# One core of Trainium2: where the row maxima are transposed between two thirds of the keys' product in an attention phase

## The chip, the cores and the metric

The kernel runs on one core of a Trainium2 chip. The metric is the device time of one execution in microseconds (us).

## The reference, cut to what matters

A decoder layer on x of shape (4, 512, 512): causal attention with 16 heads of 32, a first expert layer chosen by token id, a second expert layer with a router (2 of 8) beside a shared one, each with a residual and a layer norm. The change lies in the attention:

```python
qkv = x @ w_attn + b_attn
q, k, v = jnp.split(qkv, 3, axis=2)
...
att = jnp.einsum('bhqd,bhkd->bhqk', q, k) * (1.0 / np.sqrt(hs))
att = jnp.where(causal, att, -jnp.inf)
att = jax.nn.softmax(att, axis=-1)
y = jnp.einsum('bhqk,bhkd->bhqd', att, v)
...
x = _layernorm(x + _L0_attn_ref(x, L0_attn_w_attn, L0_attn_b_attn, L0_attn_w_proj, L0_attn_b_proj), axis=-1)
```

## The kernel before

The attention is cut into 16 groups of four heads of one batch element (NG = B * G = 16; group g belongs to batch element g // 4). Each product in float32 is made of three parts with numbers split in a high and a low half (hi x hi, lo x hi, hi x lo), four matmuls of 128x512 each, so a product has three thirds ("parts" 0, 1, 2), all at L482.

The order of the whole phase is one list of steps that attention_steps writes out. Every engine walks the same list and issues its own share of each step, so the order of each engine follows from the list, and semaphores join them. The kinds of step that matter here:

- **Q, K** (group g, part): the product of queries or keys into a bank of psT. After the last part ScalarE adds the bias and rounds to the high half (L624, ch_hi), VectorE subtracts to get the low half (L766, ch_lo) and frees the bank. Then 12 DMA copies (L362, on the sync engine's queue; for the keys of the first three groups some are issued by ScalarE, L631 and L635) bring the halves into the stacks qS and kS of the group. There are three of each stack, but one ch_hi and one ch_lo, with a half for Q and a half for K. ScalarE overwrites the Q half for group g only when all copies of group g - 1 have landed (stack_in).
- **P1** (group, unit u = 0 to 9): the scores, queries down the partitions, into psS (L548); VectorE masks them and takes the row maxima (L782). The first unit of a group waits for the landing of its stack, each later one for the maxima of the unit two before.
- **M** (group): four transposes of the row maxima into four rows of a psT bank (L556). ScalarE writes them, negated, as four more rows of qS (L642).
- **P2** (group, unit): scores again, keys down the partitions, with the maxima subtracted by those four rows, into psE (L569); ScalarE's exponential (L652); GpSimd's causal mask (L424).
- **PV** (group, j): numerators and denominators into psO and psN (L587). NORM and YH divide and split the result. V, PR, XT, CW, LN1, LN2 (L833), ST, LZ and ZB are the values' product, the output product with its layer norm and stores, the loads of the residual and the transposes of weights for the next phase.

XT, Q, K, V, PR, M and CW share the two banks of psT by turns: every use takes the other bank from the one before, in the order of the list (a product at its part 0), and waits until the last use of that bank is read (sh_free).

Pass s of the loop (16 of them) runs P1 of group s + 1 beside P2 of group s and PV of group s - 1. Its start, called "head s" in this document, is made of the six parts of Q and K of group s + 2; from the fourth on, a unit of P1 of group s + 1 stands after each, and M of group s stands after one of them. In the heads 14 and 15 there is no product of that kind, and M follows two units of P1, or none.

After the head come four PV steps (from s = 1 on) with units of P1 and P2 between, then the remaining units spread over V or PR products. The fourth pass of each batch element and the third have no such product to fill with.

The two waits that the step M has on TensorE:

```python
elif kind == "M":
    g = s[1]
    out = take(s)
    pe.wait_ge(max_done, UNITS * (g + 1))
    for t in range(QT):
        last = pe.transpose(out[0:4, t * P:(t + 1) * P], rowmax[:, g % 2, t, :], ident[:])
```

Of the kernel before, what the change touches and what calls it, by code (L numbers as in the profile page):

```python
# [24 lines left out]
def attention_steps(B, QT, NG):  # L25

    def product(kind, *at):
        return [(kind, *at, part) for part in range(3)]

    def spread(slots, extra):  # L30
        out, taken = [], 0
        for n, s in enumerate(slots):
            out += s
            upto = len(extra) * (n + 1) // len(slots)
            out += extra[taken:upto]
            taken = upto
        return out

    steps = []
    for i in range(QT):  # L40
        steps += [("XT", 0, i)]
    steps += product("Q", 0) + product("K", 0) + [("RT1",)]
    steps += product("V", 0, 0) + [("CNT",), ("RT2", 0)] + product("V", 0, 1) + product("V", 0, 2)
    steps += spread([[("P1", 0, u)] for u in range(10)], product("Q", 1) + product("K", 1) + product("V", 0, 3))
    order = (0, 1, 3, 2)
    left = []
    for s in range(NG):
        b, at = s // 4, s % 4
        fill, early, soon = [], [], []
        if at == 0 and b:  # L50
            for i in range(QT):
                fill += product("V", b, i)
        if at == 1:
            turn = [("XT", b + 1, i) for i in range(QT)] if b + 1 < B else []
            out = [product("PR", b - 1, i) for i in range(QT)] if b else [[]] * QT
            fill += (out[0] + out[1] + out[2] + turn[2:] + out[3]) if b else []
            early = turn[:2]
            soon = [] if b else turn[2:]
            if b:
                fill += [("LN1", b - 1, i) for i in range(QT)]  # L60
        if s == NG - 2:
            fill += [("CW", n) for n in range(5)]
        if s == NG - 1:
            fill += [("CW", n) for n in range(5, 9)]
        head = product("Q", s + 2) + product("K", s + 2) if s + 2 < NG else []
        p1 = [("P1", s + 1, u) for u in range(10)] if s + 1 < NG else []
        p2 = [("P2", s, u) for u in range(10)]
        norm = [("NORM", s - 1, n) for n in range(3)] if s else []

        for n, one in enumerate(head):  # L70
            if (s, n) == (1, 1):
                steps += [("RT3",)]
            steps += [one] + left[n:n + 1] + (p1[n - 3:n - 2] if n >= 3 else [])
            if n == 3:
                steps += [("M", s)]
        if not head:
            steps += p1[:2] + [("M", s)]
            p1 = p1[2:]
        else:
            p1 = p1[3:]  # L80
        if s:
            for n, j in enumerate(order):
                steps += [("PV", s - 1, j)] + p1[n:n + 1] + p2[n:n + 1] + early[n:n + 1]
                if s == NG - 2 and n < 2:
                    for i in (2 * n, 2 * n + 1):
                        steps += [("LN2", b - 1, i), ("ST", b - 1, i)]
                if s == NG - 1:
                    steps += [("ZB", b, n)]
                if n == 1 and at == 3 and b and b < B - 1:
                    steps += [("LZ", b)]  # L90
            p1, p2 = p1[4:], p2[4:]
        p2 = [x for pair in zip(p1, p2) for x in pair] + p2[len(p1):]
        keep = 0 if len(fill) > 4 or s == NG - 1 else 3
        left = p2[len(p2) - keep:]
        p2 = p2[:len(p2) - keep]
        slots = []
        for m, one in enumerate(p2):
            one = [one] + norm[m:m + 1] + soon[m:m + 1]
            if m in (6, 9) and s == 0:
                one += [("RT2", 1 + m // 9)]  # L100
            slots += [one]
        slots[-1] += norm[len(p2):]
        steps += spread(slots, fill)
        if s:
            steps += [("YH", s - 1)]
        if s == NG - 2:
            steps += [("LZ", B - 1)]
        elif at == 2 and b:
            for i in range(QT):
                steps += [("LN2", b - 1, i), ("ST", b - 1, i)]  # L110
        if at == 3 and b < B - 1:
            steps += [("ZB", b, i) for i in range(QT)]
    b = B - 1
    steps += [("DR",)] + [("PV", NG - 1, j) for j in order] + [("NH", 0), ("CW", 9), ("NH", 1)]
    steps += product("PR", b, 0) + product("PR", b, 1) + [("LN1", b, 0)]
    steps += product("PR", b, 2) + [("LN2", b, 0), ("LN1", b, 1), ("ST", b, 0)]
    steps += product("PR", b, 3) + [("LN1", b, 2), ("LN2", b, 1), ("LN1", b, 3), ("ST", b, 1)]
    for i in (2, 3):
        steps += [("LN2", b, i), ("ST", b, i)]
    steps += [("CW", n) for n in range(10, 16)]  # L120
    return steps


def attention_phase(nc, sems, acc, store, ident, powm, xs_in, pos, table, packed, place, number, x, w_attn, b_attn, w_proj, b_proj, tokens, ctx_w, sorted_x1, sorted_x2):
# [14 lines left out]
    NS = table.shape[2]  # L139

    steps = attention_steps(B, QT, NG)

    SHARED = ("XT", "Q", "K", "V", "PR", "M", "CW", "CNT")
# [1966 lines left out]
```

## Time and profile before

| what | value |
|---|---|
| median of 3 runs | 1259.26 us (1259.04 to 1263.15) |
| the profiled execution's own time | 1274.87 us |
| its span | 1273.1 us |
| its mean granted TensorE clock | 0.969 of full |
| attention phase, from the timeline | to about 457 us |
| PE busy | 1192.2 us, 94% |
| PE's part of the chain that ended last | 70% |

A busy PE in this table means that a matmul is in its pipeline. Idle time of an engine counts only where it stands in the chain that ended last. Timeline rows give the start, the length, the engine, the line and, in brackets, how long the engine was idle before and what released it. "PEld" is the load of the stationary operand, which runs ahead of the matmul. A row with x8 or x4 merges several instructions.

### The profile page before, as it was taken

The page shows a single profiled execution, that of the slowest core. Times are in us where ns is not written, and L with a number is a line of the kernel's source. Part 1 is how long each engine was busy: PE and PEld are TensorE (multiplying, and loading weights), DVE is VectorE, ACT ScalarE, POOL GpSimd, SP SyncE. Part 2 cuts the span into 40 slices and gives each one's busy share as a digit, 9 for nine tenths or more (in the row PEclk, how much of TensorE's full clock was granted, in tenths as well). Part 3 has the DMA queues.
Part 4 walks back from the last instruction along what each step waited for, and adds up shares of the span by engine and source line. Part 5 has one row for each costly group of instructions (what it writes and reads, how often), then busy time and mean ns, then how long its engine had stood idle before and what let it go on. Part 6 is the DMA issues. An engine that isn't in the chain of part 4 may idle for free.

```text
span 1273.1 us, 20255 instructions
## 1 busy us (share of the span) xinstructions
PE 1192.2 (94%) x6404; PEld 936.2 (74%) x6404; DVE 686.3 (54%) x1485; ACT 454.6 (36%) x699; POOL 282.0 (22%) x405
## 2 busy tenths in 40 slices
PE   7788999999899879999899999999999998999996
PEld 6565576576566558887587888899999997778884
DVE  5574556556557546775355634343443432676744
ACT  3154334433434422332242334244444433333331
POOL 3022313412514410223121540000000000443302
PEclk8889999899899979999899999999999999999998
DMA  7346563532523324333055665245345432655530
GB/s 246 79 111 225 176 230 120 144 82 55 137 56 115 100 83 133 124 110 130 26 75 93 214 225 191 82 146 184 127 131 195 152 99 67 195 179 172 174 116 33
DMA packets 128815, 169.76 MB, mean 133 GB/s; under 512 B 18113, under 2 KB 71361, under 8 KB 128705
## 3 DMA queue, kind: packets, MB, share of 16 engines
q1 hardware_dynamic: 113056, 132.45, 35.2%
q0 software_dynamic: 10336, 32.53, 7.2%
q10 hardware_dynamic: 5312, 3.42, 1.2%
q8 instruction: 56, 0.92, 0.3%
q14 instruction: 55, 0.44, 0.1%
HBM read 95.98 MB, written 47.19 MB: 112 GB/s over the span
## 4 chain that ended last, share of the span: by engine, by line
PE 70%; DVE 8%; DMA 6%; SPq 6%; issue 3%; ACT 2%; POOL 2%; ACTq 1%; POOLq 0%; DVEq 0%
PE bank L847 26%; PE bank L908 13%; PE psT L482 11%; SPq L362 5%; PE psS L548 2%; PE bank L1528 2%; PE psO L587 2%; PE bank L1529 2%; PE bank L1530 2%; DMA shared_raw<-in_L_ffn_Sd_dram 2%; PE psN L587 2%; PE psE L569 2%; PE bank L1550 1%; PE bank L1573 1%; DVE psS L782 1%
## 5 line engine op out<-in xcount | busy, mean ns | idle before, releaser
L908 PE MATMUL bank<-store,shared_held 128*128 128x512 f32 x792 | 188.1, 393 | 3.5 <-issue 2.9
L908 PEld LDWEIGHTS bank<-store,shared_held 128*128 128x128 f32 x792 | 149.0, 189 | 38.5 <-DVE shared_held L1847 4.2
L482 PE MATMUL psT<-store 128*128 128x512 f32 x576 | 164.3, 422 | 5.2 <-DVE store L696 3.5
L782 DVE CUSTOM_DVE_ANT_0 psS<-psS,attn_mask 128x512 f32<-128x512 f32 (+3 forms) x256 | 120.9, 511 | 66.0 <-PE psS L548 66.0
L652 ACT ACTIVATE acc<-psE 128x512 f32<-128x512 f32 x160 | 93.7, 598 | 143.5 <-PE psE L569 140.0
L482 PEld LDWEIGHTS psT<-store 128*128 128x128 f32 x576 | 110.2, 203 | 26.4 <-issue 3.9
L1442 POOL DMA_INDIRECT routed_rows_io<-sorted_y,routed_pos x32 | 37.2, 1161 | 377.2 <-DMA sorted_y<-routed_rows_io 313.6
L424 POOL TENSOR_SCALAR_AFFINE_SELECT acc<-acc 128x256 f32<-128x256 f32 (+1 forms) x160 | 57.3, 364 | 282.0 <-ACT acc L652 281.6
L847 PE MATMUL bank<-shared_held,routed_h_hi 128*128 x624 | 115.9, 328 | 0.4 <-DVE routed_h_lo L1888 0.4
L847 PEld LDWEIGHTS bank<-shared_held,routed_h_hi 128*128 128x128 f32 x624 | 100.2, 188 | 1.4 <-issue 1.2
L847 PE MATMUL bank<-store 128*128 x351 | 91.6, 405 | 0.0
L548 PE MATMUL psS<-attn_kS,attn_qS 96*128 96x512 f32 (+3 forms) x256 | 75.9, 360 | 15.1 <-DMA attn_kS<-attn_ch_hi 7.1
L548 PEld LDWEIGHTS psS<-attn_kS,attn_qS 96*128 96x128 f32 x256 | 45.8, 199 | 56.6 <-issue 20.3
L847 PEld LDWEIGHTS bank<-store 128*128 128x128 f32 x351 | 63.6, 190 | 12.2
L569 PE MATMUL psE<-attn_qS,attn_kS 100*128 100x512 f32 (+3 forms) x256 | 69.6, 336 | 2.3 <-ACT acc L652 2.1
L1649 ACT ACTIVATE routed_h_f<-bank 128x512 f32<-128x512 f32 x44 | 26.3, 597 | 126.3 <-PE bank L908 123.2
L1528 PE MATMUL bank<-shared_held,routed_h_hi 128*128 128x512 f32 x176 | 69.8, 396 | 0.1
L1529 PE MATMUL bank<-shared_held,routed_h_hi 128*128 128x512 f32 x176 | 69.5, 395 | 0.0
L1530 PE MATMUL bank<-shared_held,routed_h_lo 128*128 128x512 f32 x176 | 69.2, 393 | 0.0
L908 PE MATMUL bank<-shared_held 128*128 128x512 f32 x264 | 65.5, 402 | 3.2 <-DVE shared_held L1847 3.1
L1847 DVE TENSOR_TENSOR shared_held<-shared_raw,shared_held 128x1024 fp32r<-128x1024 f32 x42 | 51.3, 1221 | 28.9 <-ACT shared_held L1636 28.8
L847 PE MATMUL bank<-shared_held,routed_h_lo 128*128 x312 | 62.7, 323 | 0.0
(273 smaller groups left out, 2001.4 us busy)
## 6 DMA issues: line engine op xcount, KB each, us to landing
sorted_x<-attn_zero SPq DMA_DIRECT2D x19, 768.0 KB, 6.2
shared_raw<-in_L_ffn_Sg_dram SPq DMA_DIRECT2D x44, 256.0 KB
shared_raw<-in_L_ffn_Su_dram SPq DMA_DIRECT2D x44, 256.0 KB
shared_raw<-in_L_ffn_Sd_dram SPq DMA_DIRECT2D x44, 256.0 KB
routed_rows_io<-sorted_x SPq DMA_DIRECT2D x39, 256.0 KB, 3.0
sorted_y<-routed_rows_io SPq DMA_DIRECT2D x39, 256.0 KB, 2.3
attn_qS<-attn_ch_hi SPq DMA_DIRECT2D x128, 64.0 KB
attn_kS<-attn_ch_hi SPq DMA_DIRECT2D x112, 64.0 KB
```

The source lines that it names most:

```text
L362: sp.dma_start(dst[r * D:(r + 1) * D, i, :].bitcast(F32), part[i * D:(i + 1) * D, qk, :].bitcast(F32)).then_inc(stack_in, 16)
L424: pool.affine_select(out=at, in_=at, compare_op=ALU.is_ge, fill=drop, base=0, pattern=[[0, at.shape[1]], [1, P]], channel_multiplier=-1).t ...
L482: last = pe.matmul(out, lhs[a](k), rhs[c](k), start=(s[-1] == 0 and k == 0), stop=(s[-1] == 2 and k == KC - 1))
L548: last = pe.matmul(psS[:, n % 2, c0:c0 + (t + 1) * P], q[0:AUX, i, t * P:(t + 1) * P], k[0:AUX, i, 0:(t + 1) * P], start=True, stop=True)
L569: last = pe.matmul(psE[:, n % 2, c0:c0 + (QT - j) * P], k[0:AUX + 4, i, j * P:(j + 1) * P], q[0:AUX + 4, i, j * P:T], start=True, stop=True)
L652: act.activation(p_f[:, u, :], psE[:, n % 2, :], ACT.Exp, scale=SCALE).then_inc(exp_done, 1)
L782: last = dve.tensor_tensor_reduce(scores, scores, mask[:, (3 - t) * P:T], 1.0, BELOW_ALL, ALU.add, ALU.max, rowmax[:, g % 2, t, i:i + 1])
L847: last = pe.matmul(out, lhs[a](k), rhs[c](k), start=(n == 0), stop=(n == 3 * chunks - 1))
L908: last = pe.matmul(out, w[:, slot, at + k * P:at + (k + 1) * P], x_part(k), start=(g == 0 and k == 0), stop=(g == 2 and k == KC - 1))
L1528: pe.matmul(s_y[i], h[0], w[0], start=(c == 0), stop=False)
L1529: pe.matmul(s_y[i], h[0], w[1], start=False, stop=False)
L1530: last = pe.matmul(s_y[i], h[1], w[0], start=False, stop=(c == CH - 1))
```

## The change

M of group s is written into the list after part 1 of the keys' product (n = 4) and the second unit of P1, and no longer after part 0 (n = 3) and the first unit.

```diff
@@ -71,7 +71,7 @@
             if (s, n) == (1, 1):
                 steps += [("RT3",)]
             steps += [one] + left[n:n + 1] + (p1[n - 3:n - 2] if n >= 3 else [])
-            if n == 3:
+            if n == 4:
                 steps += [("M", s)]
         if not head:
             steps += p1[:2] + [("M", s)]
```

TensorE, head 6 (L482 is a third of the keys' product, L548 a unit of scores of group 7, L556 the row maxima of group 6):

```order
 L482 MATMUL psT<-store 128x512 x16
 L548 MATMUL psS<-attn_kS,attn_qS 128x512
+L482 MATMUL psT<-store 128x512 x4
+L548 MATMUL psS<-attn_kS,attn_qS 128x512
 L556 MATMUL psT<-ident,attn_rowmax 4x128 x4
-L482 MATMUL psT<-store 128x512 x4
-L548 MATMUL psS<-attn_kS,attn_qS 128x512
 L482 MATMUL psT<-store 128x512 x4
 L548 MATMUL psS<-attn_kS,attn_qS 128x512
```

The transposes moved behind four products and one unit of scores. The same piece stands in each of the heads 0 to 13.

TensorE, head 0, where no PV step follows (L569 is the first unit of P2):

```order
 L482 MATMUL psT<-store 128x512 x20
 L548 MATMUL psS<-attn_kS,attn_qS 128x512
+L482 MATMUL psT<-store 128x512 x4
+L548 MATMUL psS<-attn_kS,attn_qS 128x512
 L556 MATMUL psT<-ident,attn_rowmax 4x128 x4
-L482 MATMUL psT<-store 128x512 x4
-L548 MATMUL psS<-attn_kS,attn_qS 128x512
 L482 MATMUL psT<-store 128x512 x4
 L548 MATMUL psS<-attn_kS,attn_qS 128x512 x2
 L569 MATMUL psE<-attn_qS,attn_kS 128x512
```

Between M and L569 there are now one third of a product and two units of scores, where there were two thirds and three units.

ScalarE, head 2, the same before and in the change (L624 for Q, one exponential of the group before, L642 for M, L624 for K):

```order
50 L624 ACTIVATE attn_ch_hi<-psT,attn_bqk 128x512 [waits attn_stack_in,attn_sh_full1]
51 L652 ACTIVATE acc<-psE 128x512 [waits attn_e_full]
52 L642 ACTIVATE attn_qS<-psT 4x2048 [waits attn_sh_full1]
53 L624 ACTIVATE attn_ch_hi<-psT,attn_bqk 128x512 [waits attn_sh_full0]
54 L652 ACTIVATE acc<-psE 128x512 [waits attn_pv_done,attn_e_full]
```

Those of the other heads read alike. Nothing moved, on ScalarE as on VectorE, GpSimd and the sync engine: L642 stands ahead of the keys' L624 in both.

## Rows read from the trace of the kernel before

**Rows 1.** The page: busy time, and TensorE's granted clock in 40 slices

```profile
PE 1192.2 (94%) x6404; PEld 936.2 (74%) x6404; DVE 686.3 (54%) x1485; ACT 454.6 (36%) x699; POOL 282.0 (22%) x405
...
PEclk8889999899899979999899999999999999999998
```

**Rows 2.** Chain that ended last, 50 to 460 us: start us, us, what

```profile
120.91 1.38 SPq L362
...
164.70 4.58 PE psT L482 x20
...
235.96 4.42 DMA attn_kS<-attn_ch_hi
...
320.11 2.75 DVE attn_z L833 x4
```

**Rows 3.** Waits: engine, line, waited for; us in total, times, longest

```profile
PEld psT L556 <- DVE attn_ch_lo L766: 15.6, 14, 1.8
...
PE psT L556 <- DVE attn_ch_lo L766: 10.3, 14, 1.4
```

**Rows 4.** Timeline of head 6, 200 to 208 us

```profile
201.34 0.39 PE L548 MATMUL psS<-attn_kS,attn_qS 96*128 96x512 f32 x1
201.36 0.75 DVE L766 SCALAR_TENSOR_TENSOR attn_ch_lo<-psT,attn_bqk,attn_ch_hi 128x512 fp32r<-128x512 f32 x1 [1.40 <-ACT attn_ch_hi L624]
...
202.17 0.60 PE L556 MATMUL psT<-ident,attn_rowmax 128*4 128x128 f32 x4 [0.43 <-DVE attn_ch_lo L766]
...
202.52 1.18 PE L482 MATMUL psT<-store 128*128 128x512 f32 x4
...
202.80 1.87 ACT L642 ACTIVATE attn_qS<-psT 4x2048 fp32r<-4x2048 f32 x1 [1.47 <-PE psT L556]
...
203.54 0.40 PE L548 MATMUL psS<-attn_kS,attn_qS 96*128 96x512 f32 x1
...
203.77 1.09 PE L482 MATMUL psT<-store 128*128 128x512 f32 x4
...
204.70 0.39 PE L548 MATMUL psS<-attn_kS,attn_qS 96*128 96x512 f32 x1
204.90 0.69 ACT L624 ACTIVATE attn_ch_hi<-psT,attn_bqk 128x512 fp32r<-128x512 f32 x1 [0.23 <-PE psT L482]
...
205.62 0.75 DVE L766 SCALAR_TENSOR_TENSOR attn_ch_lo<-psT,attn_bqk,attn_ch_hi 128x512 fp32r<-128x512 f32 x1 [0.89 <-ACT attn_ch_hi L624]
...
207.21 0.40 PE L569 MATMUL psE<-attn_qS,attn_kS 100*128 100x512 f32 x1
```

**Rows 5.** Timeline, TensorE: the transposes of heads 1 and 2

```profile
76.83 0.60 PE L556 MATMUL psT<-ident,attn_rowmax 128*4 128x128 f32 x4 [0.22 <-DVE attn_ch_lo L766]
...
97.69 0.60 PE L556 MATMUL psT<-ident,attn_rowmax 128*4 128x128 f32 x4 [0.16 <-DVE attn_ch_lo L766]
```

**Rows 6.** Timeline of TensorE, head 8

```profile
240.42 0.50 PE L548 MATMUL psS<-attn_kS,attn_qS 96*128 96x512 f32 x1 [1.49 <-DMA attn_kS<-attn_ch_hi]
241.99 1.01 PE L556 MATMUL psT<-ident,attn_rowmax 128*4 128x128 f32 x4 [1.07 <-DVE attn_ch_lo L766]
242.65 2.06 PE L482 MATMUL psT<-store 128*128 128x512 f32 x4
...
246.64 0.63 PE L548 MATMUL psS<-attn_kS,attn_qS 96*128 96x512 f32 x1
```

**Rows 7.** Timeline: the first unit of scores in heads 3, 4, 7 and 12

```profile
117.36 0.50 PE L548 MATMUL psS<-attn_kS,attn_qS 96*128 96x512 f32 x1 [2.10 <-DMA attn_kS<-attn_ch_hi]
...
139.34 0.50 PE L548 MATMUL psS<-attn_kS,attn_qS 96*128 96x512 f32 x1 [1.68 <-DMA attn_kS<-attn_ch_hi]
...
219.84 0.19 PEld L548 LDWEIGHTS psS<-attn_kS,attn_qS 96*128 96x128 f32 x1 [0.57 <-DMA attn_kS<-attn_ch_hi]
...
342.99 0.50 PE L548 MATMUL psS<-attn_kS,attn_qS 96*128 96x512 f32 x1 [1.88 <-DMA attn_kS<-attn_ch_hi]
```

**Rows 8.** Timeline: SP's stack copies of group 9, first and last (24 in all)

```profile
221.38 5.03 SPq L362 DMA_DIRECT2D attn_qS<-attn_ch_hi  x8
...
234.06 2.49 SPq L362 DMA_DIRECT2D attn_kS<-attn_ch_hi  x4
```

**Rows 9.** Stretches: us, busy by engine, granted clock, DMA share, GB/s

```profile
336.00:356.00 20.00, 17.06 (x101) 10.02 (x103) 8.64 (x27) 7.38 (x11) 8.72 (x12) 0.83 0.46 115
```

## The prediction

> **What bounds the kernel now.** I read the page first. TensorE (PE) is busy for 94% of the span, but its clock line has dips, most of them in the attention phase, the first 457 of 1273 us (14 slices and a part) [rows 1]. Everything the change touches runs there, so the question is which wait ends last in each head of that phase. (By a head I mean, as above, the start of pass s; "head 6" is that of s = 6.)
>
> The second view was the chain that ended last, cut to the attention phase [rows 2]. Three kinds of piece stand in it: long runs of PE's products; stretches of the sync engine's DMA queue (SPq, the stack copies of L362) and the flight of the last such copy; and four vector-engine (DVE) operations of L833. So the bound alternates between PE and the loop that copies Q and K into the stacks.
>
> The third view was the table of waits. PE idles 10.3 us in front of the row-maxima transposes of L556, in 14 heads, always until DVE has subtracted at L766; its weight loads idle 15.6 us there, of which the 10.3 are part [rows 3]. The cause is in the timeline of head 6 [rows 4]: M takes the psT bank that the queries' product has just filled. That bank is free only when ScalarE (ACT) has copied it (L624) and DVE has subtracted (L766, 201.36 + 0.75 = 202.11). PE gets there after one third of the keys' product and one unit of scores, at about 201.57, and stands until 202.17.
>
> By head the 14 waits are 1.07 us in heads 0, 3, 4, 7, 8 and 12 (the longer wait of head 8 is in [rows 6]); 0.43 in heads 5, 6, 9, 10 and 13; 0.22 and 0.16 in heads 1 and 2 [rows 5]; 1.38 in head 11, the longest [rows 3], where DVE was still at L833. They add up to 10.3. The waits of 1.07 are long because ACT may overwrite the Q half of ch_hi only when the previous stack has landed, which is also what the first unit of scores waits for, so both start at the same moment: the heads 3, 4, 8 and 12 wait 1.49 to 2.10 us for the landing, head 7 only 0.57 by its weight load [rows 6, 7].
>
> **The change, part by part.** Nothing is added or removed. On PE alone M moves behind four products and one unit of scores, in 14 of 16 heads. The banks stay: K takes its bank at its first third, before M in both orders. ACT, DVE, POOL and SP keep their orders.
>
> (a) *The wait.* In head 6 the steps between P1 units cost, start to start [rows 4]: a unit of scores 203.54 to 203.77 = 0.23; a third of a product 203.77 to 204.70 = 0.93; M 202.17 to 202.52 = 0.35; the third after it 202.52 to 203.54 = 1.02. In the new order, with no wait, the way from the first to the third unit of scores is 0.23 + 0.93 + 0.23 + 0.35 + 1.02 = 2.76 us; now it is 204.70 - 201.34 = 3.36. So a head gains 0.60 where the wait says 0.43: 0.17 is PE's pipeline running empty. In head 8 the first unit is followed by M after 241.99 - 240.42 = 1.57 where 0.34 would do: 1.23 against 1.07, again 0.16. I take the wait plus 0.16 for each head. PE comes to M 1.16 us later than now, so the 0.43 heads have slack; in the 1.07 heads PE arrives 0.34 + 0.93 + 0.23 = 1.50 after the first unit and the bank is free at 1.57, so nothing or 0.07 is left. All 14 heads: 10.3 + 14 x 0.16 = 12.5 us of PE time.
>
> (b) *What the stack loop takes back.* The landing that a head s waits for was started by DVE's L766 for the queries in head s-1, ahead of that head's M. After head 7's L766 SP issues from 221.38 to 234.06 + 2.49 = 236.55, about 0.63 us for each of 24 copies [rows 8], and the data are there at 240.42. PE's saving in head 7 does not move any of this. So wherever head s waits for the landing, the gain of head s-1 is gone: it turns into a longer DMA wait. That takes the gains of head 2 (0.32), 3 (1.23), 6 (0.59), 7 (1.23) and 11 (1.54), 4.9 us together. Head 10's is kept: head 11 is not held by the landing but by L833 on DVE, which follows PE's work [rows 2].
>
> (c) *Head 0.* It has no PV products between M and the first unit of P2, and the keys' copies of this pass are issued by ACT itself. M now comes right before the last third of K, and ACT's negation of it takes 1.87 us [rows 4], so ACT's L624 for the keys starts when that ends, not when the product does. I take 0.5 us, between 0 and 1.23.
>
> (d) *Cover of the later M.* Its one reader is ACT's L642. Put head 6 into the new order: M at 202.73, L642 from 203.4 to 205.3, so K's L624 starts at 205.3 instead of 204.90 and L766 ends near 206.8 instead of 206.37. Who waits? P2's first unit, now at 207.21 and then at 206.6, needs L642's end, 205.3: free. Score unit 4, two PV steps on, needs DVE's maximum of unit 2, ready about 0.7 after L766: free. SP comes to K's copies only after 12 issues x 0.63 = 7.6 us from 202.14, at 209.7: free by 2.9 us. I cost it at nothing; if this cover failed it is the slower rival below.
>
> **Sum.** Kept are heads 0 (0.5), 1 (0.38), 4, 8 and 12 (1.23 each), 5, 9, 10 and 13 (0.59 each): 0.5 + 0.38 + 3.69 + 2.36 = 6.9 us. The phases behind attention start from its last store and shift with it. The profiled execution took 1274.87 us (span 1273.1), so it would be 1268.0; it is 15.6 us above the median of the runs, which I take to be unrelated to the edit, and take the same 6.9 off the median: **1252.4 us**.
>
> **The clock.** In heads 8 and 12 PE's clock drops to its lower level (1.2 GHz) just behind the two gaps: the four products after M take 2.06 us [rows 6] against 1.18 [rows 4]; the stretch from 336 to 356 us has a granted clock of 0.83 [rows 9]. Head 4 has part of that. Before the drop PE had been idle 1.49 + 1.07 us with one unit of scores between. In the new order head 8's DMA wait grows by the 0.59 and 1.23 taken back, to 3.3 us in one piece, and M's gap is gone. Idle time in sum is no less, so I expect the low stretch to stay, and put nothing in the sum.
> The Trainium skill, "TensorE: Matmul & The Clock Gate", Part 1, says that the array is throttled by default, falls to half rate after idling and is released by sustained activity. By that rule a head without the second gap might recover sooner or never fall; that is the second rival.
>
> **The rivals.**
> 1. *The stack loop does not take back its part* (12.5 kept). For: the loop's slack is small (0.57 us at head 7) and an execution without the profiler may have faster copies. Against: four heads wait 1.5 us and more. It gives 1259.26 - 12.5 = 1246.8. Chance 0.08.
> 2. *The clock stays high in heads 4, 8 and 12.* Head 8 then needs 2.9 us from first to third unit instead of the present 246.64 - 240.42 = 6.22, so 3.3 instead of 1.23; two such heads give 2.1 each more, head 4 some 1.2: 5.4 in sum, 1247.0. Against: the longer DMA wait. Chance 0.12.
> 3. *Taken back further on.* Something not driven by PE (DVE's backlog, POOL's loads and stores of z, or the expert weights' transposes in the last two heads) absorbs half or more of the 6.9: between 1255.8 and 1259.3, no change to measure. Nothing in the chain shows such an anchor, but the end of the phase passes through POOL and DMA pieces. Chance 0.18.
> 4. *Slower: the later L642 pushes K's eviction.* ACT works in order; if K's L624, 0.4 us late by (d), reached PE through DVE's row maxima or SP's K copies, each of 14 heads would be 0.4 us longer than now: +5.6, 1264.9. It decides where K's L766 ends after SP's twelfth issue or PE's fifth unit; the slack is 2.9 us by the first. Chance 0.05.
> 5. *The edit does not do what it says*: excluded by the listings, which show M moved in 14 heads and no bank or wait changed.
>
> **How the numbers follow.** Forecast 0.57, rivals as above. About 0.3% (3.8 us, 1255.5) is what a measurement of this kernel can tell from no change. Forecast and rivals 1 and 2 lie beyond it, except for a small part of the forecast's own spread (head 0, and half of the kept heads by chance caught by a landing): faster 0.74, same 0.20, slower 0.06. The range reaches from rivals 1 and 2 up into rival 3: 1246.5 to 1258.0.
>
> **What would show it.** In the profile of the changed kernel PE's wait at L556 should fall from 10.3 us to under 1, save for heads 14 and 15, which are unchanged. The waits of L548 for the stack copies in heads 3, 4, 7, 8 and 12 should grow by 0.3, 1.2, 0.6, 1.2 and 1.5 us and more; the interval from head 4 to head 5 should shrink by 1.2, that from 7 to 8 not at all. The low clock at heads 8 and 12 stays. K's L624 waits for L642, not for the product. The forecast is wrong if L548's waits grow by the whole 10 us, or if new idle time stands before L569 or L548's later units.

## The result, and the profile after

| | before | changed |
|---|---|---|
| median | 1263.49 us (20 runs, 1259.04 to 1268.04) | 1255.99 us (20 runs, 1250.52 to 1259.55) |
| ratio, changed to before | | 0.9935, 95% interval 0.9922 to 0.9948 |
| span of the profiled execution | 1273.1 us | 1252.6 us |
| start of the next phase (L1010) in it | 460.25 us | 446.72 us |

The change makes the kernel 8.2 us faster (0.0065 x 1263.5; by the interval 6.6 to 9.9; the two medians lie 7.5 apart). 20.5 us lie between the two profiled executions, 13.5 of them up to the start of the next phase. No run shows the rest to be the change's: from L1010 to the end the profiled spans of all the kernels below lie between 805 and 813 us, with 806 and 807 in two that move M in only two or three heads, and no instruction differs there.

The page of the changed kernel, to be read against [rows 1]: PE is 8 us less busy for the same 6404 matmuls, and in the clock's line the eighth and the eleventh slice, which hold heads 8 and 12, rose from 8 to 9, while the fifth, with head 4, fell from 9 to 8. The second and the twentieth rose too, and the twentieth lies far behind the attention. (Slices are 31.8 us before and 31.3 now.)

```profile
PE 1184.2 (95%) x6404; PEld 934.3 (75%) x6404; DVE 684.8 (55%) x1485; ACT 454.6 (36%) x699; POOL 281.0 (22%) x405
...
PEclk8989899999999979999999999999999999999998
```

The waits of the changed kernel that answer to [rows 3] (engine, line, waited for: us in total, times, longest). PE itself no longer waits for L766 at L556; of 15.6 us of its weight loads 2.1 are left. The waits for copies grew, from 7.1 us (4 times) to 8.9 (5 times) on PE: 1.8 where I had expected some 4.9. In a second profile of each kernel they are 4.3 and 7.8 us.

```profile
PE psS L548 <- DMA attn_kS<-attn_ch_hi: 8.9, 5, 3.3
...
PEld psT L556 <- DVE attn_ch_lo L766: 2.1, 6, 0.6
...
PE psE L569 <- ACT attn_qS L642: 0.5, 1, 0.5
```

Head 6 of the changed kernel, its timeline, answering to [rows 4]. The first to third unit of scores take 201.81 - 199.06 = 2.75 us, where they took 3.36.

```profile
199.06 0.40 PE L548 MATMUL psS<-attn_kS,attn_qS 96*128 96x512 f32 x1
199.08 0.75 DVE L766 SCALAR_TENSOR_TENSOR attn_ch_lo<-psT,attn_bqk,attn_ch_hi 128x512 fp32r<-128x512 f32 x1 [1.43 <-ACT attn_ch_hi L624]
...
200.45 0.60 PE L556 MATMUL psT<-ident,attn_rowmax 128*4 128x128 f32 x4
...
201.09 1.86 ACT L642 ACTIVATE attn_qS<-psT 4x2048 fp32r<-4x2048 f32 x1 [2.04 <-PE psT L556]
201.81 0.39 PE L548 MATMUL psS<-attn_kS,attn_qS 96*128 96x512 f32 x1
202.98 0.69 ACT L624 ACTIVATE attn_ch_hi<-psT,attn_bqk 128x512 fp32r<-128x512 f32 x1
...
204.32 0.40 PE L569 MATMUL psE<-attn_qS,attn_kS 100*128 100x512 f32 x1
```

Head 8 of the changed kernel, TensorE, answering to [rows 6]. The transposes take 0.60 us, not 1.01, and the third behind them 1.17, not 2.06: the clock has stayed at its upper level. The first to third unit take 239.63 - 236.71 = 2.92 us instead of 6.22.

```profile
236.71 0.50 PE L548 MATMUL psS<-attn_kS,attn_qS 96*128 96x512 f32 x1 [1.39 <-DMA attn_kS<-attn_ch_hi]
...
238.27 0.60 PE L556 MATMUL psT<-ident,attn_rowmax 128*4 128x128 f32 x4
238.63 1.17 PE L482 MATMUL psT<-store 128*128 128x512 f32 x4
239.63 0.40 PE L548 MATMUL psS<-attn_kS,attn_qS 96*128 96x512 f32 x1
```

The stretches between the first units of scores of successive heads show where the time went. Each entry is the difference of the starts of two such rows; the second columns come from a second profile of either kernel, taken in the runs told below.

| heads | before | before, 2nd | changed | changed, 2nd | forecast change |
|---|---|---|---|---|---|
| 0 to 1 | 22.13 | 22.14 | 21.37 | 21.02 | -0.5 |
| 1 to 2 | 20.92 | 22.44 | 20.57 | 22.24 | -0.38 |
| 2 to 3 | 20.23 | 19.14 | 21.07 | 19.36 | 0 |
| 3 to 4 | 21.98 | 21.35 | 22.12 | 21.75 | 0 |
| 4 to 5 | 30.66 | 30.69 | 30.77 | 30.43 | -1.23 |
| 5 to 6 | 31.34 | 31.33 | 30.75 | 30.78 | -0.59 |
| 6 to 7 | 18.50 | 18.17 | 18.32 | 18.41 | 0 |
| 7 to 8 | 20.58 | 20.20 | 19.33 | 19.21 | 0 |
| 8 to 9 | 31.84 | 30.63 | 27.99 | 27.99 | -1.23 |
| 9 to 10 | 31.34 | 31.33 | 30.79 | 30.77 | -0.59 |
| 10 to 11 | 18.20 | 18.19 | 17.58 | 17.59 | -0.59 |
| 11 to 12 | 21.19 | 19.52 | 19.05 | 18.54 | 0 |
| 12 to 13 | 31.73 | 29.15 | 28.01 | 28.00 | -1.23 |

Three things ask for a test: that heads 2, 3 and 6 gave nothing; that 7 and 11 gave something; and that 8 and 12 gave more than their wait, while 4 gave less.

### The profile page after: what moved, and what is told of

Read it like the earlier page. It is cut to its first block, busy times and chain, and to the rows that moved or that the text cites. A ratio compares the mean times of both kernels' runs of the same rounds, so it can differ in the third digit from the quotient of the medians.

```text
span 1252.6 us, 20255 instructions
## 1 busy us (share of the span) xinstructions
PE 1184.2 (95%) x6404; PEld 934.3 (75%) x6404; DVE 684.8 (55%) x1485; ACT 454.6 (36%) x699; POOL 281.0 (22%) x405
## 4 chain that ended last, share of the span: by engine, by line
PE 68%; DVE 8%; SPq 7%; DMA 7%; POOL 3%; issue 3%; ACT 2%; ACTq 2%; POOLq 0%; DVEq 0%
PE bank L847 26%; PE bank L908 12%; PE psT L482 11%; SPq L362 6%; DMA shared_raw<-in_L_ffn_Sd_dram 3%; PE psS L548 2%; PE bank L1528 2%; PE bank L1529 2%; PE bank L1530 2%; PE psO L587 2%; PE psE L569 2%; PE psN L587 2%; POOL routed_rows_io L1442 1%; PE bank L1550 1%; DVE shared_held L1847 1%
## 5 line engine op out<-in xcount | busy, mean ns | idle before, releaser
L482 PE MATMUL psT<-store 128*128 128x512 f32 x576 | 158.9, 411 | 5.4 <-DVE store L696 3.5
L482 PEld LDWEIGHTS psT<-store 128*128 128x128 f32 x576 | 106.6, 196 | 25.0 <-issue 4.0
L548 PE MATMUL psS<-attn_kS,attn_qS 96*128 96x512 f32 (+3 forms) x256 | 74.8, 356 | 17.3 <-DMA attn_kS<-attn_ch_hi 8.9
L548 PEld LDWEIGHTS psS<-attn_kS,attn_qS 96*128 96x128 f32 x256 | 45.3, 197 | 58.4 <-DVE attn_rowmax L782 21.9
L569 PE MATMUL psE<-attn_qS,attn_kS 100*128 100x512 f32 (+3 forms) x256 | 70.1, 339 | 2.3 <-ACT acc L652 1.6
L766 DVE SCALAR_TENSOR_TENSOR attn_ch_lo<-psT,attn_bqk,attn_ch_hi 128x512 fp32r<-128x512 f32 x32 | 24.0, 751 | 74.2 <-ACT attn_ch_hi L624 70.3
```

The costliest lines, as they stand in the source:

```text
L482: last = pe.matmul(out, lhs[a](k), rhs[c](k), start=(s[-1] == 0 and k == 0), stop=(s[-1] == 2 and k == KC - 1))
L548: last = pe.matmul(psS[:, n % 2, c0:c0 + (t + 1) * P], q[0:AUX, i, t * P:(t + 1) * P], k[0:AUX, i, 0:(t + 1) * P], start=True, stop=True)
L569: last = pe.matmul(psE[:, n % 2, c0:c0 + (QT - j) * P], k[0:AUX + 4, i, j * P:(j + 1) * P], q[0:AUX + 4, i, j * P:T], start=True, stop=True)
```

## Experiment 1: the moved step in some heads only

The theories were A, the prediction's (the landing of the stack copies hangs only on L766 of the head before, and takes back what heads 2, 3, 6, 7 and 11 save); B (the last copies share the DMA engines with the 1 MB load of z, L459, which moves with PE); and the clock (M's gap right behind the landing gap is what lets the clock fall). Kernels with M moved in a choice of heads:

```diff
-            if n == 3:
+            if n == (4 if s in (2, 3, 6) else 3):
```

> M moved in heads 2, 3 and 6 alone. Theory A (stack loop): head s's landing hangs on the queries' L766 of head s-1, so what these heads save (0.3, 1.2, 0.6 us) comes back as longer waits of L548 for the copies in heads 3, 4 and 7; the interval from the first unit of scores of head 3 to that of head 4 stays at 21.98 us within 0.3, and the time is that of before within 1 us. Rival (landings follow PE's work too): head 4 comes 1 us sooner or more, time 2 us shorter. Theory of the clock: no effect on heads 8 and 12, which stay at the low level behind their gaps (M's transposes merge to 1.01 us there).

```diff
-            if n == 3:
+            if n == (4 if s in (7, 11) else 3):
```

> M moved in heads 7 and 11 alone. Theory A: head 8's landing hangs on the queries' L766 of head 7 alone, 19.06 us ahead of it as before; interval from head 7's to head 8's first unit of scores stays 20.6 us, no gain in time. Theory B (the last copies share the DMA engines with the 1 MB load of z, L459, which POOL issues behind PE's PV steps and which moves with PE): the interval falls by 1.1 to 1.3 us in head 8, and by 1.3 to 1.6 in head 12; together 2.5 us of time. Heads 8 and 12 keep M right behind the landing: if the low clock there comes from the two gaps together it stays (M 1.01 us).

```diff
-            if n == 3:
+            if n == (3 if s in (2, 3, 6, 7, 11) else 4):
```

> M moved in heads 0, 1, 4, 5, 8, 9, 10, 12 and 13, the ones that the prediction called kept. Theory A: the whole gain of the change as forecast, 6.9 us, with nothing lost against the full change. Theory B: 6.9 us, and the full change is some 2.7 us faster than this one. Theory of the clock (the second gap of heads 8 and 12 is what lets it fall): M's transposes in heads 8 and 12 take 0.60 us and not 1.01, and each of these heads gives 2.1 us more, so the profiled run gains up to 11 us. If the low clock comes by chance with either kernel, 1.01 may appear in one of the heads again.

| M moved in heads | ratio to before, 95% interval | 3 to 4 | 6 to 7 | 7 to 8 | 8 to 9 | 11 to 12 | 12 to 13 |
|---|---|---|---|---|---|---|---|
| 2, 3, 6 | 1.0020 (1.0004 to 1.0037) | 21.97 | 18.25 | 20.12 | 29.16 | 21.61 | 30.73 |
| 7, 11 | 0.9988 (0.9972 to 1.0003) | 21.81 | 18.35 | 19.39 | 30.65 | 18.77 | 30.67 |
| the other nine | 0.9947 (0.9928 to 0.9967) | 21.48 | 18.26 | 19.91 | 27.99 | 21.60 | 28.01 |

*Heads 2, 3 and 6 alone* give nothing; by the interval they even lose a little. The timeline of that kernel shows PE's saving of head 3 standing as idle time in front of head 4:

```profile
119.06 0.50 PE L548 MATMUL psS<-attn_kS,attn_qS 96*128 96x512 f32 x1 [1.39 <-DMA attn_kS<-attn_ch_hi]
...
120.62 0.60 PE L556 MATMUL psT<-ident,attn_rowmax 128*4 128x128 f32 x4
...
141.03 0.79 PE L548 MATMUL psS<-attn_kS,attn_qS 96*128 96x512 f32 x1 [4.04 <-DMA attn_kS<-attn_ch_hi]
```

141.03 - 119.06 = 21.97 us, as in the kernel before (21.98, 21.35): theory A holds for the heads whose copies have SP's issues as their bound.

*Heads 7 and 11 alone* shorten exactly their own two stretches: 7 to 8 from 20.58, 20.20, 20.12 and 19.91 (four profiles with M unmoved in head 7) to 19.39, and 11 to 12 to 18.77, where the unmoved ones have 21.19, 19.52, 21.61 and 21.60. A is wrong for these two heads. In time it is 1.5 us, with an interval that reaches no change.

*The other nine* carry most of the gain, 6.7 us (4.2 to 9.1); its 8 to 9 and 12 to 13 are those of the changed kernel. Theory B had the full change 2.7 us faster than this kernel; by the ratios it is 1.5 us, and the intervals overlap, so the timed runs don't tell A from B. The stretches do.

## Experiment 2: the load of z

In the changed kernel L459 is issued at 226.33, 7.43 us after L766 of head 7 has ended (218.15 + 0.75); in the kernel before at 229.94, 8.58 us after it (220.61 + 0.75). The timelines of the two, POOL's and SP's queue, before and then changed:

```profile
229.94 0.85 POOL L459 DMA_DIRECT2D attn_z<-in_x_dram  x1
```

```profile
226.33 0.85 POOL L459 DMA_DIRECT2D attn_z<-in_x_dram  x1
...
231.62 3.60 SPq L362 DMA_DIRECT2D attn_kS<-attn_ch_hi  x4
```

SP's last copy is issued by 236.55 before [rows 8] and by 235.22 in the changed kernel; the stack is there at 240.42 and at 236.71. So the flight of the last copies falls from 3.9 to 1.5 us. Part of this is only moved: those last four copies now take 3.60 us to issue and not 2.49. In the second profiles the flight is 3.1 us before and 2.6 in the changed kernel. What both pairs show is the whole way from SP's first copy of group 9 to the landing: 19.04 and 18.29 us before, 17.78 and 17.67 changed. The load (7.0 and 6.6 us from issue to landing, the middle one of three such loads) leaves earlier by what PE saves, and should be through at about 232.9, before the last copies are all issued. To test it, the load alone was moved, one PV step sooner and two later, with M where it was before:

```diff
-                if n == 1 and at == 3 and b and b < B - 1:
+                if n == 0 and at == 3 and b and b < B - 1:
```

> M where it was before; POOL issues the 1 MB load of z in the fourth pass of batch elements 1 and 2 one PV step sooner (about 2 us). Theory B (this load delays the last stack copies): the interval from the first unit of scores of head 7 to that of head 8 falls from 20.58 us (19.9 to 20.6 in three runs with M unmoved there) to about 19.3, that from head 11 to 12 from 21.2 to 21.6 down to about 19; 1.5 to 3.5 us of time. Theory A (only the queries' L766 and SP's issues): no change, within 0.3 us. Rival C: the load waits for the stores of z to land and POOL stands still, so the mask of PV's step 1 comes late and PE waits at L587 in heads 7 and 11.

```diff
-                if n == 1 and at == 3 and b and b < B - 1:
+                if n == 3 and at == 3 and b and b < B - 1:
```

> The same load two PV steps later (about 3 us), M where it was before. Theory B: its flight lies fully over the keys' last copies and behind them, head 8's and head 12's landing come later: intervals 7 to 8 and 11 to 12 grow by 0.5 to 3 us, time 1 to 5 us longer. Theory A: no change of the intervals. Rival: the copies get ahead of the load and land sooner, intervals of 18 to 19 us.

| load of z | issued | after SP's first copy of group 9 | landing after that copy | 7 to 8 | 11 to 12 | ratio to before |
|---|---|---|---|---|---|---|
| one step sooner | 228.36 | 6.9 | 17.35 | 19.27 | 19.28 | 0.9978 (0.9955 to 1.0000) |
| as before (two profiles) | 229.94, 230.93 | 8.6, 8.5 | 19.04, 18.29 | 20.58, 20.20 | 21.19, 19.52 | 1 |
| two steps later | 232.48 | 11.6 | 19.85 | 21.39 | 21.27 | 1.0080 (1.0052 to 1.0109) |

The kernels of experiment 1 fit in: with M unmoved in head 7 the load leaves 8.6 us after that copy and the stack lands after 18.58 and 18.25 us; with M moved in heads 7 and 11 it is 7.4 and 17.79, as in the changed kernel.

The first unit of scores of head 8, with the load sooner and then later (timelines of TensorE):

```profile
238.86 0.47 PE L548 MATMUL psS<-attn_kS,attn_qS 96*128 96x512 f32 x1
```

```profile
240.75 0.49 PE L548 MATMUL psS<-attn_kS,attn_qS 96*128 96x512 f32 x1 [2.31 <-DMA attn_kS<-attn_ch_hi]
```

With M unmoved, the earlier load alone takes PE's landing wait away, and the later one lengthens it: theory B is shown for head 8, in both directions. For head 12 the later load stays inside what the unmoved kernels show (19.52 to 21.61), and the earlier one lies only 0.24 us below them, so it is not shown there by itself. The later load costs 10 us in time, more than the two stretches explain (1.0 us on the mean of before at head 8). Its profile doesn't show the rest: from head 0 to L1010 it takes 404.3 us, and the kernel before 403.9 on the mean of two. Where the rest goes stays open. The Trainium skill, "DMA: Bandwidth & Descriptors", "Issuing engines are not separate DMA queues", says that DMAs started by different engines run on the same 16 DMA engines and interleave. The trace agrees: as POOL's load is issued 6.9, 8.6 or 11.6 us after SP's first copy, SP's stack lands after 17.35, 19.04 or 19.85 us.

## Experiment 3: the clock

> The kernel before, unchanged, for a second profile. Theory of the clock (M's own gap behind the landing gap is what drops it): M's transposes in heads 8 and 12 merge to more than 0.60 us in most profiles of this order, as in the first (1.01 and 1.01). If this profile shows 0.60 in both, the low clock of the first profile was chance, and the 3.8 us that each of these heads gave in the first pair is not the change's doing beyond 1.2.

> The changed kernel, unchanged, on the chip of the two above, for a second profile. Theory of the clock: M's transposes in heads 8 and 12 take 0.60 us and the intervals 8 to 9 and 12 to 13 are 28.0 us, as in the first profile of it. If either is 30 us or more, the high clock there is chance too. Theory A in heads 3 and 4: L548 waits there for the landing by more than in the kernel before (about 3.3 and 2.7 us), the interval 3 to 4 stays about 22 us.

The second profile of the kernel before fell to the lower clock in head 8 (1.01 us) and not in head 12 (0.60). The second of the changed kernel had 0.60 in both. Counting the stretches 8 to 9 and 12 to 13 of all profiles by whether M was moved in head 8 or 12: with M moved (eight profiles, 16 stretches, those of the last two sections among them) 14 take 27.92 to 28.01 us, and two, both in head 8, take 29.5. With M unmoved (six profiles, 12 stretches) five take 29.07 to 29.16, and seven 30.63 to 31.84, with the transposes merging to 0.70 or 1.01 us in six of these seven. So:

- the wait itself is worth 29.1 - 28.0 = 1.1 us in each of these heads, against 1.23 forecast;
- a fall of the clock behind it costs another 1.5 to 2.7 us. It happened in 7 of 12 with the second gap, and in 2 of 16 without. The means are 30.2 and 28.2: 2.0 us a head, not 1.23.

Head 4 goes the other way. Its stretch is 30.5 to 31.3 us in all six profiles with M unmoved there. The clock falls in head 4 before the change too: in the first profile the granted clock is still 1.00 in the microsecond to 141.34, two behind the first unit of scores, and 0.50 from 142.34 to 145.34. With M moved in it, the stretch is 28.0 in the kernel where head 3's M had not moved (wait 2.37 us, granted clock 1.00 throughout), and 30.77 and 30.43 in the changed kernel. There PE idles for longer in front of head 4 (2.68 and 3.82 us, against 1.68 and 2.25), and the clock falls within that gap (0.71 in its last microsecond in the first profile) and stays at 0.50 until 143.54, six microseconds and not three. The timeline of the changed kernel:

```profile
137.54 0.80 PE L548 MATMUL psS<-attn_kS,attn_qS 96*128 96x512 f32 x1 [2.68 <-DMA attn_kS<-attn_ch_hi]
138.14 1.91 PE L482 MATMUL psT<-store 128*128 128x512 f32 x4
...
140.27 1.05 PE L556 MATMUL psT<-ident,attn_rowmax 128*4 128x128 f32 x4
140.98 2.05 PE L482 MATMUL psT<-store 128*128 128x512 f32 x4
```

Four products take 1.91 and 2.05 us, against 1.08 and 1.17 in head 8. What head 3 saves comes back in head 4 twice: as a wait, and as a clock that falls sooner and stays low for longer, which uses up what head 4's own move saves. The first is shown by experiment 1. The second rests on the one kernel with head 3 unmoved and on those of the last section, in which the wait in front of head 4 is short (0.8 to 1.5 us), and all give 28.0; no run changed that wait alone.

## Experiment 4: M behind the last third

```diff
-            if n == 3:
+            if n == 5:
```

> M behind the last third of K (n = 5) in heads 0 to 13. ScalarE's L624 for the keys then stands ahead of L642. PE's wait at L556 is 0 as in the change, so no further gain there. Cover of the later M: the first unit of P2 needs L642 (1.87 us) after L624 (0.69): in heads 1 to 13 M ends about 0.4 us before PV's first step (1.9 us) and a unit of scores (0.3), so P2 would wait some 0.3 to 0.8 us per head; in head 0 2 us. Expected time: that of the change or up to 8 us above it, still below before. If the cover is larger than thought, the same as the change within 2 us.

Measured: 0.9959 (0.9939 to 0.9979), where the change has 0.9935 (0.9922 to 0.9948); the two intervals overlap. In heads 1 to 13 no new wait stands in front of P2, where 0.3 to 0.8 us a head had been expected. In head 0 one does, of 5.17 us where 2 had been expected. ScalarE, which issues the keys' copies of this pass itself (L635), puts them ahead of L642; the stretch 0 to 1 takes 23.28 us where the changed kernel has 21.37 and 21.02. TensorE and ScalarE in head 0 of this kernel:

```profile
66.24 0.80 PE L569 MATMUL psE<-attn_qS,attn_kS 100*128 100x512 f32 x1 [5.17 <-ACT attn_qS L642]
```

```profile
61.70 2.58 ACTq L635 DMA_DIRECT2D attn_kS<-attn_ch_lo  x4
64.32 1.86 ACT L642 ACTIVATE attn_qS<-psT 4x2048 fp32r<-4x2048 f32 x1 [3.44 <-issue]
```

ScalarE and TensorE in head 6:

```profile
206.41 0.69 ACT L624 ACTIVATE attn_ch_hi<-psT,attn_bqk 128x512 fp32r<-128x512 f32 x1 [2.54 <-PE psT L482]
207.12 1.86 ACT L642 ACTIVATE attn_qS<-psT 4x2048 fp32r<-4x2048 f32 x1
```

```profile
203.89 0.40 PE L548 MATMUL psS<-attn_kS,attn_qS 96*128 96x512 f32 x1
...
209.16 0.39 PE L569 MATMUL psE<-attn_qS,attn_kS 100*128 100x512 f32 x1
```

L642 ends at 208.98 and P2 begins at 209.16, 5.27 us after the head's first unit of scores; in the changed kernel it is 204.32 - 199.06 = 5.26. The cover ends just there. Its 8 to 9 and 12 to 13 are 27.92 and 27.97. Two other stretches grew, 6 to 7 to 19.29 and 10 to 11 to 18.50 (18.32 and 17.58 in the changed kernel): SP's first eight copies take 5.9 us to issue in these two heads and not 5.0, for a reason that stays open. One more place gains nothing, uses the cover up, and in head 0 goes beyond it.

## Experiment 5: what holds heads 3 and 4, and a faster version

In the chain of the changed kernel SP's copies stand where the zero-fills (L332, 768 KB each) drain. Two fills instead of four behind each group:

```diff
-                        for _ in range(min(4, len(pieces))):
+                        for _ in range(min(2, len(pieces))):
```

> The change, and two instead of four zero-fills (768 KB each) behind each group's stack copies on SP. In heads 3 and 4 the eight copies of ch_hi behind the fills take 8 us to issue instead of 5, which is in the chain. Expected: the intervals from head 2 to 3 and 3 to 4 (21.1 and 22.1 in the change) fall by 1 to 2.5 us each, later ones where fills now run (heads 6 to 10) grow by less than 0.5; 2 to 4 us faster than the change, ratio to before about 0.991. Rival: the fills only move the delay to other groups, and the time is that of the change.

Measured: 0.9942 (0.9921 to 0.9964), no gain over the change; the rival was right. The stretches 2 to 3, 3 to 4 and 4 to 5 fell to 18.51, 19.38 and 28.00 us, as expected, but 7 to 8 rose to 21.72 and 11 to 12 to 20.53, and in head 8 the clock fell. SP's queue in this kernel, head 7:

```profile
210.89 1.14 SPq L332 DMA_DIRECT2D sorted_x<-attn_zero  x2
213.88 7.41 SPq L362 DMA_DIRECT2D attn_qS<-attn_ch_hi  x8
```

Eight copies take 7.4 us to issue here, and 5.0 in [rows 8]. The two fills are not all of it: in heads 2 to 4 of this kernel eight copies behind two fills take 5.5 to 5.6 us. In head 7 POOL's scattered stores (L452, from 211.28) leave at the same time. So the fills were put only where the next copies have a long pass:

```diff
-                    if g >= 3 and qk == 1:
-                        for _ in range(min(4, len(pieces))):
+                    if g in (5, 6, 7) and qk == 1:
+                        for _ in range(min((4, 8, 8)[g - 5], len(pieces))):
```

> The change, and the 19 zero-fills issued behind the stack copies of groups 5, 6 and 7 (4, 8, 7) instead of 3 to 7 (4, 4, 4, 4, 3), so that none drains while the copies for heads 3, 4, 8 or 12 are issued. Expected from the profile of the variant with two fills: intervals 2 to 3 and 3 to 4 of 18.5 and 19.4 us or less instead of 21.1 and 22.1, 4 to 5 28.0 instead of 30.8 as the clock stays up, and 7 to 8 19.3 as in the change, not 21.7. That is 5 us without the clock, up to 8 with it: ratio to before 0.987 to 0.990. Rival: eight fills in a row hold up the copies of groups 7 and 8, and head 7 waits for its landing 1 us and more longer.

The next kernel is this one with the load of z one PV step sooner as well, by the diff of experiment 2:

> The same, and the 1 MB load of z one PV step sooner. With M unmoved that made 7 to 8 and 11 to 12 19.3 us. With M moved, PE is 1.2 us further at the load, so a further step gives: intervals 18 to 19 us instead of 19.3 and 19.05, up to 1.5 us in sum. Rival: the load cannot start before the stores of z have landed, and nothing is gained over the variant without it.

Measured: 0.9958 (0.9938 to 0.9977) and 0.9923 (0.9896 to 0.9949). Heads 3 and 4 did what was expected (18.21, 19.14 and 27.99 in the first, 17.86, 18.71 and 28.00 in the second), and head 7 gave back 7.4 us (6 to 7 took 25.74 and 25.85). The stretch 7 to 8 took 20.80 us in the first, where 19.3 had been expected, and 19.33 in the second, with 18.44 for 11 to 12. By the times the two are not told apart. The rival was right and its size far too small, 8 us and not 1. TensorE and SP's queue in the first:

```profile
218.88 0.80 PE L548 MATMUL psS<-attn_kS,attn_qS 96*128 96x512 f32 x1 [7.97 <-DMA attn_kS<-attn_ch_hi]
```

```profile
186.25 9.37 SPq L332 DMA_DIRECT2D sorted_x<-attn_zero  x8
195.73 9.98 SPq L362 DMA_DIRECT2D attn_qS<-attn_ch_hi  x8
```

The fills behind group 7 were more than the pass behind them could take (there are 20 in all, not 19, so eight stood here): SP comes to group 8's copies only at 195.73, and then issues eight of them in 10 us. From 190 to 205 us this kernel's DMA engines are busy throughout:

```profile
190.00:200.00 10.00, 10.00 (x64) 5.86 (x62) 5.83 (x19) 4.88 (x7) 4.48 (x8) 1.00 1.03 376
200.00:205.00 5.00, 4.87 (x52) 3.17 (x49) 3.03 (x15) 2.17 (x4) 0.88 (x3) 1.00 1.03 366
```

(The columns are those of [rows 9]: share of the DMA engines 1.03, 376 and 366 GB/s.) The last kernel moves five fills on, behind group 10:

```diff
-                    if g in (5, 6, 7) and qk == 1:
-                        for _ in range(min((4, 8, 8)[g - 5], len(pieces))):
+                    if g in (5, 6, 7, 10) and qk == 1:
+                        for _ in range({5: 4, 6: 8, 7: 3, 10: 5}[g]):
```

> The variant with placed fills and the earlier load of z, with the eight fills behind group 7's copies cut to three and five moved behind group 10's, where the next copies have 30 us of time (4, 8, 3 and 5 fills, 20 in all; the earlier runs counted 19, as the page does). If the wait of 8 us in head 7 came from the eight fills that drain while group 8's copies are issued, it is gone: interval 6 to 7 of 18.4 us instead of 25.8, the others as there (17.9, 18.7, 28.0, 19.3, 17.6, 18.4), 7.4 us faster than that run: ratio to before about 0.987. Rival: the earlier load of z or the slower DMA queue is what holds head 7, and 6 to 7 stays over 22 us; or eight fills behind group 6 do the same to group 7's copies and head 6 waits.

Measured: median 1246.23 us against 1260.26 for the kernel before beside it, ratio 0.9887 (0.9856 to 0.9918): faster than both kernels, by 14 us against before and, by the ratios, about 6 us against the change (the two intervals, up to 0.9918 and from 0.9922, just don't meet). No run has these four places for the fills without the earlier load of z, so what each of the two gives is not shown. The stretch 6 to 7 is 18.77 us, and head 7's wait 1.01:

```profile
208.85 0.51 PE L548 MATMUL psS<-attn_kS,attn_qS 96*128 96x512 f32 x1 [1.01 <-DMA attn_kS<-attn_ch_hi]
```

The eight fills behind group 6 did no harm (5 to 6 30.78 us). One stretch missed: 8 to 9 took 29.51, with the lower clock in head 8 behind a wait of 1.69 us.

## Why the prediction was right, and where it was not

The forecast was a gain of 6.9 us and 1252.4 us; measured are 8.2 us (6.6 to 9.9) and 1255.99, inside the range. The time came out 3.6 above the forecast because the median of the kernel before was 1263.49 over 20 runs and not 1259.26.

- *(a) The wait.* Right, and well sized. First to third unit in head 6: 2.76 forecast, 2.75 measured. The 0.59 of heads 5, 9 and 10 is 0.57, 0.55 and 0.61 by the stretches.
- *(b) The stack loop.* Right for heads 2, 3 and 6, as the kernel with these three alone shows. Wrong for heads 7 and 11, and the step that failed is the sentence "PE's saving in head 7 does not move any of this". It holds for the moment at which SP begins, but the landing at 240.42 came 3.9 us after the last issue, and I didn't ask what filled that flight. It was a load that POOL issues behind PE's own steps; as it leaves 1.2 us sooner, SP's first copy and the landing lie 17.78 us apart and not 19.04. The saving there is 1.1 us at head 7 and 1.6 at head 11 (means of two profiles each); [rows 2] had the 4.42 us in it.
- *(c) Head 0.* 0.5 of a possible 1.23 was put in. In the two pairs 0 to 1 fell by 0.9, but the other four profiles with M unmoved in head 0 have 21.07, 21.18, 21.14 and 23.06 there, so its size is not shown. What is shown is the mechanism: L569 waits 0.55 us for L642, and 5.17 us when M goes one place further (experiment 4).
- *(d) The cover.* Right to 0.04 us in head 6: L624 of the keys follows its head's first unit by 3.92 us (forecast 3.96), P2 by 5.26 (forecast 5.26, 206.6 - 201.34). The slower rival never had its condition.
- *The clock.* The sentence "I expect the low stretch to stay" failed for heads 8 and 12. It leaned on head 8's wait growing to 3.3 us in one piece. That sum was wrong in itself, as it takes in the 0.59 of head 6, which (b) gives to head 7's wait; (b) makes it 1.49 + 1.23 = 2.7. By (b)'s error it did not grow at all (1.49 before, 1.39 after; 0.76 and 1.27 in the second profiles). So rival 2 came in for two of its three heads, with 0.8 us a head more than the wait on the mean of all profiles, not 2.1, since the kernel before does not always fall there. In head 4 the growth did happen, and with it a fall of the clock that came sooner and lasted longer: 1.23 forecast, about 0.1 measured.
- *The signs named in advance.* PE's wait at L556 for L766 is gone, as forecast, and the keys' L624 follows L642 directly. The waits of L548 were to grow by 0.3, 1.2, 0.6, 1.2 and 1.5 us in heads 3, 4, 7, 8 and 12; in the first pair they changed by +1.2, +1.0, +0.6, -0.1 and -1.0. The stretch 4 to 5 was to shrink by 1.2 and did not; 7 to 8 was to stay and shrank.

By stretches the two errors, +2.7 for heads 7 and 11 and +1.6 for the clock in 8 and 12, less 1.1 in head 4, would make 6.9 into 10.1. That the forecast came within 1.3 us of the measured gain is in part luck: it left out gains at four heads and a loss at one, and the timed runs show less than the stretches do.

The profiled pairs show 11.2 us from head 0 to L1010 (means of two each: 403.9 and 392.7); the timed runs show 8.2 with 9.9 as the upper end. Why timed runs gain less than profiled ones is open. They have no trace, and the clock and the flights, in which two profiles of one kernel differ by up to 2.6 us a stretch, are a likely place, which no run tests.

## What to carry to other kernels

A wait that is moved off the path is worth its length up to the next wait that hangs on something else. So walk back from each such wait to what starts it, the flight of a DMA after its last issue included, and ask what else was in flight and which engine released that. Where the trace shows a bulk transfer ahead of small copies that a loop depends on, its place in the program is worth a look too: here placing the fills and the load of z went with some 6 us on top of the 8, and other places for the fills gave nothing. And a gap on TensorE has a second price behind it, the lower clock, which depends on the other gap next to it.

## What the runs showed of the hardware

- Bulk transfers slow the *issue* of small ones on the same queue. Eight copies of 64 KB by SP take about 5.0 us in the heads with no fill in flight (5.9 in two heads of the kernel with M behind the last third), 5.5 to 5.6 behind two fills of 768 KB (7.4 with POOL's scattered stores beside them), 6.7 to 8.0 behind four, and 10.0 and 11.0 behind eight, with the DMA engines at 366 to 376 GB/s.
- A 1 MB load from another queue delays the landing of small copies by where it falls. From SP's first copy to the landing of all 24 it is 17.4 us with the load 6.9 us behind that copy, 17.7 to 17.8 with 7.4, 18.3 to 19.0 with 8.6 and 19.9 with 11.6.
- TensorE's clock, at 1.2 in place of 2.4 GHz: behind an idle stretch, one unit of scores and another idle 1.07 us it fell in seven cases, with first stretches of 0.64 to 2.31 us, and not in five, with 0 to 1.83; in the kernel before it fell with 0.76 and 1.49 in head 8 and, in head 12, with 1.88 and not with 0.27. Behind idle time in one piece the length alone does not tell: 1.39 did not bring it down in the changed kernel, nor did 2.32 in head 12 of the kernel with nine heads moved and 2.42 in head 12 of the one with two fills, while 1.69 did in the last kernel; 2.68, 3.80, 3.82 and 7.97 did.
